# ScalarE rounds each rotated query or key tile one period later, between the probabilities' high parts and the next exponentials

## What is computed

```
q = (hidden_states @ Wq.T).reshape(b, s, H, HD).transpose(0, 2, 1, 3)
k = (hidden_states @ Wk.T).reshape(b, s, KVH, HD).transpose(0, 2, 1, 3)
v = (hidden_states @ Wv.T).reshape(b, s, KVH, HD).transpose(0, 2, 1, 3)
apply_rope = lambda x: x * cos + _rotate_half(x) * sin
q = apply_rope(q)
k = apply_rope(k)
logits = jnp.einsum('bhqd,bhkd->bhqk', q, k) * scale
logits = jnp.where(causal, logits, jnp.finfo(dtype).min)
attn = jax.nn.softmax(logits, axis=-1)
out = jnp.einsum('bhqk,bhkd->bhqd', attn, v)
return out @ Wo.T
```

## Time and profile before

| | |
|---|---|
| median of 3 runs | 455.61 us (455.09, 455.61, 459.3) |
| the profiled execution, its own time | 454.57 us |
| its span in the profile | 452.8 us |
| granted clock of PE | 0.999 of full speed |
| PE busy | 426.0 us (94%) |
| PE's weight loads busy | 307.1 us (68%) |
| DVE / ACT / POOL busy | 361.0 / 349.4 / 341.8 us |

### The profile page before, as it was taken

The page is one execution under the profiler, slowest core; times in us unless marked ns, Lnnn a source line. Parts: engine busy times, 40 slices in busy tenths (PEclk is TensorE's granted clock), DMA queues, the critical chain, the costliest instruction groups (busy, mean ns, idle before and its releaser), DMA issues.

```text
span 452.8 us, 12338 instructions
## 1 busy us (share of the span) xinstructions
PE 426.0 (94%) x4509; PEld 307.1 (68%) x4509; DVE 361.0 (80%) x994; ACT 349.4 (77%) x643; POOL 341.8 (76%) x306
## 2 busy tenths in 40 slices
PE   8988999899999999999999998999989988999994
PEld 4556767687877788787788886777846444554562
DVE  5978798688898889888889998988867679545666
ACT  5668999889899899989989889979855466743441
POOL 5568899997699986769999887855325795486692
PEclk9999999999999999999999999999999999999999
DMA  8475436668142694334358332364120000000001
GB/s 292 144 214 171 112 95 158 171 142 211 25 119 72 180 217 143 98 79 131 94 144 186 106 83 72 81 171 103 25 48 0 1 1 2 0 1 0 25 23 49
DMA packets 58108, 45.13 MB, mean 100 GB/s; under 512 B 36856, under 2 KB 49600, under 8 KB 58048
## 3 DMA queue, kind: packets, MB, share of 16 engines
q1 hardware_dynamic: 57440, 43.67, 36.2%
q10 hardware_dynamic: 608, 0.66, 0.4%
HBM read 23.93 MB, written 11.54 MB: 78 GB/s over the span
## 4 chain that ended last, share of the span: by engine, by line
PE 65%; POOL 13%; DVE 8%; ACT 6%; issue 5%; DMA 2%; SPq 0%; ACTq 0%; DVEq 0%; POOLq 0%
PE ps L574 11%; PE ps L489 9%; PE ps L491 9%; PE ps L490 9%; PE ps L555 5%; PE ps L557 5%; PE ps L598 3%; PE ps L602 3%; PE ps L600 3%; PE ps L816 3%; POOL raw L1668 2%; POOL rot L1668 2%; PE ps L846 2%; POOL rot L1687 2%; POOL on_l L1692 2%
## 5 line engine op out<-in xcount | busy, mean ns | idle before, releaser
L1379 DVE SCALAR_TENSOR_TENSOR pl<-ps,ph 128x512 f16<-128x512 f32 (+1 forms) x128 | 105.0, 821 | 23.1 <-ACT ph L1026 19.4
L1371 DVE CUSTOM_DVE_ANT_0 prob<-ps,causal 128x512 f32<-128x512 f32 (+3 forms) x256 | 117.4, 484 | 6.3 <-PE ps L557 5.0
L1019 ACT ACTIVATE prob<-prob,least 128x512 f32<-128x512 f32 (+3 forms) x256 | 122.3, 554 | 0.0
L1026 ACT ACTIVATE ph<-ps 128x512 f16<-128x512 f32 (+1 forms) x128 | 87.0, 700 | 22.3 <-PE ps L574 19.8
L574 PE MATMUL ps<-ident,prob 128*128 128x128 f32 x640 | 81.7, 274 | 0.7 <-DVE pl L1379 0.6
L555 PE MATMUL ps<-kT_h,qT 128*128 128x512 f16 (+3 forms) x256 | 76.1, 300 | 5.4 <-DVE least L1371 5.3
L574 PEld LDWEIGHTS ps<-ident,prob 128*128 128x128 f32 x640 | 68.9, 141 | 1.9 <-DVE pl L1379 1.3
L557 PE MATMUL ps<-kT_l,qT 128*128 128x512 f16 (+3 forms) x256 | 69.7, 299 | 0.0
L598 PE MATMUL ps<-vh,ph 128*128 128x65 f16 x640 | 64.9, 194 | 0.4 <-DVE pl L1379 0.4
L600 PE MATMUL ps<-vl,ph 128*128 128x64 f16 x640 | 64.9, 193 | 0.0
L602 PE MATMUL ps<-vh,pl 128*128 128x65 f16 x640 | 64.8, 193 | 0.0
(11 more groups left out here) (220 smaller groups left out, 996.4 us busy)
## 6 DMA issues: line engine op xcount, KB each, us to landing
spill<-rot SPq DMA_DIRECT2D x20, 512.0 KB, 3.2
wst<-chunks SPq DMA_DIRECT2D x30, 256.0 KB, 4.1
qT<-spill SPq DMA_DIRECT2D x15, 512.0 KB, 3.8
kT_h<-spill SPq DMA_DIRECT2D x6, 256.0 KB, 3.9
xs<-x SPq DMA_DIRECT2D x2, 512.0 KB, 5.6
oT<-wmod SPq DMA_DIRECT2D x2, 512.0 KB, 8.7
raw<-chunks SPq DMA_DIRECT2D x4, 256.0 KB, 4.8
out<-xs SPq DMA_DIRECT2D x4, 256.0 KB, 2.2
```

What stands on the lines that cost most here:

```text
L1019: act.activation(prob[:, m % 2, c], prob[:, m % 2, c], ACT.Exp, bias=least[:, m % 2, qt:qt + 1], scale=-1.0).then_inc(exp_done, 1)
L1371: ins = dve.tensor_tensor_reduce(prob[:, m % 2, at:at + w], ps[:, bank, off:off + w], causal[:, S - w:S], -1.0 / HD ** 0.5, 3.0e38, ALU.ad ...
L1379: dve.scalar_tensor_tensor(out=pl[:, m % 2, c], in0=ps[:, PT_BANK:PT_BANK + 3, :].rearrange("p a b -> p (a b)")[:, c], scalar=PROB_SCALE, ...
```

## The change

The call of rotated_high moves within ScalarE's loop over the periods: from behind the weight chunk of period ITEM_AT+3 to a place in period ITEM_AT+4, behind the two pieces of ph and ahead of the four exponentials. So the 17 roundings stand in periods 2, 5, 7, 10, 13, 18, 21, 23, 26, 29, 34, 37, 39, 42, 45, 50 and 53. No instruction is added or taken away, and the programs of PE, DVE, POOL and SP stay as they are.

```
                 if 0 <= n + 1 < HEADS:
                     probs_high(n + 1, 0)
                     probs_high(n + 1, 1)
+                for it in range(DIRECT, len(ITEMS)):
+                    if ITEM_AT[it] + 4 == n:
+                        rotated_high(it)
                 ended = [i for i in range(10, len(TILES)) if tile_period(i) == n]
                 if 0 <= n + 2 < HEADS:
                     exps(n + 2, (3, 2, 0, 1))
...
                 if n in SPLIT_AT[6:]:
                     chunk_high(SPLIT_AT.index(n))
-                for it in range(DIRECT, len(ITEMS)):
-                    if ITEM_AT[it] + 3 == n:
-                        rotated_high(it)
                 if n - 1 in XN2_AT:
                     second_high(XN2_AT.index(n - 1))
```

## The result

The changed kernel takes 460.3 us (median of 15 runs, 458.86 to 462.4), the kernel before 456.32 (15 runs, 455.02 to 459.3). The ratio is 1.0076, with an interval of 1.0054 to 1.0098: slower by three quarters of a per cent, where 455.5 was forecast, and outside the range of 453.2 to 458.0. The profiled execution took 459.79 us with a span of 458.0, against 452.8 before: 5.2 us to account for. The runs of the kernel before lie in two groups, 455.0 to 456.5 and 458.2 to 459.3 us, and those of the changed kernel in one.

The account below looks back on a forecast made before the run. PE was taken to set the pace, with POOL a second bound in the first third. Terms 0.0 + 0.1 - 0.75 + 0.55 = -0.1 us gave 454.5 profiled, 455.5 as median; range 453.2 to 458.0.

Parts of the forecast that it names:

- the queues that the rounding passes: POOL's low part and SyncE's spill wait for the moved rounding; scores come three periods later, so hidden by 0.9 us: 0.0.
- PE bounds the pace, and D up to 1.37 is free: In even periods, D (ph's start behind PE's transposes) costs nothing to 1.37 us, then one for one; PE sets pace.
- The rival drawn from the Trainium skill: ScalarE, not PE, sets period lengths, so falls of 0.73 us shorten four periods: -2.9 us, 452.6 us, chance 0.03.
- Periods 1 to 16: First third, POOL 1.16 us late without idle time: gain in period 10 lost again by period 14; 0.0, -1.0 to +0.9.
- Period 10: ph could start 2.2 to 2.3 us earlier, but PE waits for oT, late through POOL: gain about 1.0 us.
- Period 13: Rounding waits for late rope sums, exponentials start at 101.23 as before; period 14 loses the microsecond gained earlier.
- Period 49: Without its rounding, ph of period 50 starts earlier: gain 0.95 us, less up to 0.25 in period 51; taken as -0.75.
- Period 53: Exponentials come 0.95 us later, so ph of period 54 starts 0.56 us over its limit: +0.55, between +0.3 and +0.95.
- Period 42: One of four even periods that gain a rounding from an odd one: room for the exponentials, no gain, length stays 5.05 us.
- The transfers land late: Rival: in periods 9 and 13 PE waits 1 to 2 us each for items POOL makes late: +2, 457.5 us, chance 0.09.
- POOL's lateness is not handed on: Rival: PE keeps 2.3 us from period 10 and 0.95 from period 49: about -3, 452.6 us, chance 0.12.
- ScalarE passes the limit: Rival: ph starts too late behind odd periods that get a rounding, and from period 50: +2.2, 457.8 us, chance 0.12.

Follow-up runs that it names:

- The version with the 15 other moves: Against the kernel before, 15 of the 17 roundings moved, those of old periods 33 and 49 left in place: 456.57 us, ratio 1.0006.

## Why the prediction was wrong

**The step that failed** is the one on the queues that the rounding passes. It said that POOL's low part waits for the new place, worked out when the item would land in memory, and concluded "So this is hidden, by 0.9 us and what lies ahead of the scores in their period". The item's own readers were in time indeed. What I did not follow is what stands behind the waiting low part on POOL. I had done that for the first third, from 47.72 to 104.24, and read the absence of idle time there; I did not look for the same in the other two stretches, where it was to be read just as plainly (199.52 to 259.71, and 275.34 to the rows at 296.57). At both of their heads stands a moved rounding's low part. The Trainium skill (TensorE: Matmul & The Clock Gate, Architectural detail: the array is 16× 32×32, not 1× 128×128) notes that each of GpSimd's queues is strictly first in, first out; the trace agrees, with 2.55 us at 202.07 and again at on_l at 233.85, and 3.10 at 278.44 and 3.13 at 299.70. The term was 0.0. In its place the table above has +3.03 in periods 55 and 56, 1.37 of waiting and 1.66 of slow time behind it, and +0.95 in period 42, where POOL's lateness took 1.41 of the room and a slower landing the rest. The clock was in no term of the prediction.

Point by point:

- **PE bounds the pace, and D up to 1.37 is free.** Right. All even periods from 18 to 48 but period 42 have the length they had, six of them with D raised from between 0.64 and 0.77 to between 1.22 and 1.37. In the kernel before, PE is busy for all of the 100 us from 130 to 230. The version with the 15 other moves, 1.0006, shows it in the time as well. The rival drawn from the Trainium skill (Perfetto Trace Analysis, Identifying the Most-Contended Engine), by which each fall of D would shorten a period, did not appear: periods 18, 26 and 34, where D fell from 1.37 to 0.64, kept their 5.05.
- **Periods 1 to 16, 0.0.** Measured +1.14 at period 15, of which 0.66 came from ahead of the first moved rounding; the version with the 15 others, with 0.15 of such a start, has +0.61, so the change's own part is +0.4 to +0.5, within the term's range. But the parts were not as told. Period 2 gained 0.66, which I had not counted (its ph too stood behind a rounding), periods 3, 6 and 8 lost 1.18, period 10 gained 0.37 where I took 1.0, and period 14 lost 0.33. The first moved low part came at 49.56, not 48.88, 0.66 of it from the late start.
- **Period 10.** "About 6.4 us with PE waiting for oT" was wrong in both: 7.03, with 1.81 us of waiting for POOL's low part of the weight chunk. oT had landed at 87.14, ahead of the product at 88.24. POOL was the right engine, but not by way of oT.
- **Period 13.** Right in its end, not in its reason. Period 14 became longer, 5.55 for 5.22, with D at 1.88, not 2.5. But the rounding did not wait for the rope sums: it followed ph, which had waited for PE, without a gap (ph 100.08 + 1.47, rounding at 101.45), and the exponentials started at 102.39 in place of 101.25. The transposes of period 15, told to stay at 108.2, came at 109.39.
- **Period 49.** -0.75 taken, -0.89 measured.
- **Period 53.** +0.55 taken, +0.53 measured in periods 51 to 54, with D of period 54 at 1.47, not 1.59. 0.11 of it is in period 53 itself, which the prediction did not have.
- **Period 42** was named in the sum only as one of four with room for its exponentials. It had the room (D fell from 1.37 to 0.65) and grew by 0.95 for the transpose of on_l, issued late and landed slowly.

**The rivals.** None of them is what happened. "The transfers land late" is nearest: oT for period 42 did land late. But it spoke of items, in periods 9 and 13, and not of a queue that passes its lateness on for 20 us. "POOL's lateness is not handed on" failed in the direction of loss. "ScalarE passes the limit" is refuted by the version with the 15 other moves, which holds all its places but two and loses 0.5 us in the trace. The slower side had 0.06 by over 1%; the measured 0.76% lies within 1%, as the chances had it, and it is the range that missed.

**What stays open.** Why the transpose of period 42 took 4.3 us to land in place of 2.5: it goes with the packet of queue q8 in three of three profiles, but no run moved that packet by itself. With a landing in 2.5 us period 42 would have had no wait for it, by the times above, so the 0.95 is not the queue's lateness alone. In the version with spare work on POOL period 42 grew by 0.30 with a landing in 2.5 us, and that is not traced. The 0.39 us in the rest of the span arise behind period 62 (21.47 us from period 57 to 62, before 21.46); six versions in which the clock did not fall there have 147.73 to 147.88 for that rest, before 147.62, so it need not be the change's.

## What to carry to other kernels

When a step is moved to a later place, go through every engine that waits for it, and there not only to the reader of its result but down the queue behind the waiting instruction, to the next idle time: if there is none before another engine's need, the wait arrives there in full. POOL, 76% busy here, had two stretches of 20 to 60 us without a gap, and a wait of 1 us at the head of one was worth more than the 15 other moves together. Where PE was made to wait 2 us in period 55, the slow time behind it cost as much as the added waiting, or more. And before a late transfer is blamed for its issue alone, read its time from issue to landing in both traces.

## What the hardware showed that I had not expected

- **The clock behind a wait.** The kernels in which PE waited 2 us or more in period 55 (the changed one, and those with 7.58, 8.21 and 8.35 us in it) all show the granted clock at 0.50 behind or within it, with ten transposes at 1.97 to 2.34 us in place of 1.26, and 0.7 to 1.5 us more in period 56. The kernels with waits of 0.87, and of 0.76 + 0.88, stayed at 1.00. In period 10 PE waits 2.17 or 2.18 us in the kernel before and in four versions: in the profile of the one with only old periods 33 and 49 moved the clock was 0.72 from 92 to 96 us, in the four others it stayed. So such a wait brings it down in some executions and not in others.
- **The start.** In some executions the clock falls near the start, at different places: to 0.50 between 29.8 and 33.3 us in the changed kernel's profile, with period 2 coming 0.66 us later, and between 36.2 and 43.0 in two others, with period 2 coming 2.6 to 2.7 us later; four more lose 1.0 to 1.5 us by period 2 to a shorter such stretch behind 36 us. In the kernel before it did not fall. It is not the change's: the version with spare work on POOL, with all roundings in their old places, has it from 29.5 to 33.0. Whether this is also what parts the runs of the kernel before into two groups is not shown, since no trace of the upper group was kept.
